# Cross-attention on one core: the first three steps, the normalisation and the last step rearranged

## What is computed

```python
h = (x - mean) * rsqrt(var + 1e-5) * gamma + beta      # x: 8 x 256 x 256
Q = (h @ Wq); K = (context @ Wk); V = (context @ Wv)   # context: 8 x 256 x 192, 16 heads of 64
attn = softmax(einsum('bihd,bjhd->bhij', Q, K), axis=-1) * 64 ** -0.5
out = einsum('bhij,bjhd->bihd', attn, V).reshape(8, 256, 1024) @ Wo + bo
return x + out
```

## Time and profile before

| | |
|---|---|
| runs | 374.82, 373.36, 373.44 us; median 373.44 |
| profiled execution | 374.68 us, of which the span of its records is 372.9 us |
| TensorE (PE) | busy 356.7 us, 96% of the span |
| VectorE (DVE) | busy 245.6 us, 66% |
| ScalarE (ACT) | busy 252.6 us, 68% |
| GpSimd (POOL) | busy 161.1 us, 43% |
| transfers | 10.39 MB, mean 28 GB/s |

### The profile page before, as it was taken

The page is one execution under the profiler, slowest core; times in us unless marked ns, Lnnn a source line. Parts: engine busy times, 40 slices in busy tenths (PEclk is TensorE's granted clock), DMA queues, the critical chain, the costliest instruction groups (busy, mean ns, idle before and its releaser), DMA issues.

```text
span 372.9 us, 8902 instructions
## 1 busy us (share of the span) xinstructions
PE 356.7 (96%) x3122; PEld 308.4 (83%) x3122; DVE 245.6 (66%) x534; ACT 252.6 (68%) x757; POOL 161.1 (43%) x314
## 2 busy tenths in 40 slices
PE   5896999999999999999999999999999999999984
PEld 4776888988888888888889888889888888988863
DVE  5877576675668656595656866676665956566552
ACT  5776866677766667776667777666776766677761
POOL 6437772445532373332624445324733335333330
PEclk9998999999999999999999999999999999999999
DMA  6940010020002000020000200010000000000000
GB/s 173 262 130 1 5 49 2 0 80 1 2 2 60 20 0 0 0 77 0 0 1 0 77 0 0 0 48 29 0 0 0 28 2 0 3 2 29 3 0 30
DMA packets 10135, 10.39 MB, mean 28 GB/s; under 512 B 864, under 2 KB 9056, under 8 KB 10112
## 3 DMA queue, kind: packets, MB, share of 16 engines
q1 hardware_dynamic: 9728, 9.77, 9.1%
q0 software_dynamic: 112, 0.13, 0.4%
q10 hardware_dynamic: 272, 0.20, 0.2%
HBM read 8.00 MB, written 2.10 MB: 27 GB/s over the span
## 4 chain that ended last, share of the span: by engine, by line
PE 91%; DVE 3%; ACT 3%; POOL 1%; issue 1%; POOLq 0%; DVEq 0%
PE st_ps L705 15%; PE mix_ps L642 15%; PE o_ps L693 13%; PE st_ps L623 13%; PE w_ps L672 12%; PE w_ps L661 11%; PE w_ps L724 10%; ACT prob L381 2%; PE w_ps L606 1%; PE w_ps L598 1%; DVE qk_lo L523 1%; DVE w_lo L442 1%; PE o_ps L593 1%; POOL w_lo L264 1%; DVE neg_max L510 1%
## 5 line engine op out<-in xcount | busy, mean ns | idle before, releaser
L292 POOL TENSOR_SCALAR prob<-prob,inv 128x256 f32<-128x256 f32 x256 | 121.6, 491 | 162.2 <-DVE inv L517 162.2
L381 ACT ACTIVATE prob<-st_ps,neg_max 128x256 f32<-128x256 f32 x256 | 118.6, 474 | 26.4 <-DVE neg_max L510 26.2
L510 DVE TENSOR_REDUCE neg_max<-st_ps 128x2 f32<-128x512 f32 x128 | 82.6, 684 | 35.4 <-PE st_ps L623 35.1
L425 ACT ACTIVATE prob_t<-st_ps 128x512 f32<-128x512 f32 x64 | 38.4, 599 | 49.7 <-PE st_ps L705 49.7
L575 DVE COPY prob_t<-st_ps 128x512 f32<-128x512 f32 x64 | 44.3, 692 | 37.0 <-PE st_ps L705 33.5
L642 PE MATMUL mix_ps<-prob_t,v_sb 128*64 128x256 f32 x512 | 62.3, 385 | 0.1
L705 PE MATMUL st_ps<-ident,prob 128*128 128x128 f32 x512 | 61.8, 274 | 0.0
L705 PEld LDWEIGHTS st_ps<-ident,prob 128*128 128x128 f32 x512 | 57.4, 142 | 0.1
L523 DVE TENSOR_TENSOR qk_lo<-w_ps,qk_hi 128x512 fp32r<-128x512 f32 x64 | 44.0, 688 | 17.6 <-ACT qk_hi L391 17.1
L381 ACT ACTIVATION_READ_ACCUMULATOR prob<-st_ps,neg_max 128x1 f32 x256 | 52.8, 206 | 0.0
L642 PEld LDWEIGHTS mix_ps<-prob_t,v_sb 128*64 128x64 f32 x512 | 34.0, 136 | 18.2 <-issue 0.3
(11 more groups left out here) (70 smaller groups left out, 579.5 us busy)
## 6 DMA issues: line engine op xcount, KB each, us to landing
x_in<-in_x_dram SPq DMA_DIRECT2D x8, 256.0 KB, 3.0
out_dram<-y_sb SPq DMA_DIRECT2D x8, 256.0 KB, 2.2
c_in<-in_ctx_dram SPq DMA_DIRECT2D x7, 192.0 KB, 2.9
w_raw<-in_L_xattn_Wo_dram SPq DMA_DIRECT2D x4, 256.0 KB, 7.6
w_raw<-in_L_xattn_Wk_dram SPq DMA_DIRECT2D x4, 128.0 KB, 4.8
w_raw<-in_L_xattn_Wq_dram SPq DMA_DIRECT2D x4, 128.0 KB, 3.3
w_raw<-in_L_xattn_Wv_dram SPq DMA_DIRECT2D x2, 256.0 KB, 7.0
w_raw<-in_L_xattn_Wv_dram SPq DMA_DIRECT2D x4, 128.0 KB, 6.6
```

The lines of the kernel that those rows point to most:

```text
L292: last = nc.gpsimd.tensor_scalar(prob[:, e, r, :], prob[:, e, r, :], inv[:, e, r:r + 1], SCALE, ALU.mult, ALU.mult)
L381: last = nc.scalar.activation(prob[:, e, r, :], st_ps[e][:, r * ROWS:(r + 1) * ROWS], ACT.Exp, bias=neg_max[:, e, r:r + 1], accum_out=sums ...
L510: nc.vector.tensor_reduce(neg_max[:, e, :], st_ps[e][:, :].rearrange("p (r j) -> p r j", r=RT), AX, ALU.max, negate=True).then_inc(max_rea ...
```

## The change

Six things are different.

- The quarters of K and Q: the second half of their columns comes as two quarters, 24 pieces of weights in place of 20. More of the low parts of late pieces are made by GpSimd (`LO_POOL`), and they stand at other places in the engines' orders.
- TensorE waits for the high parts ahead of the first pass of a projection, and for the low parts only ahead of the pass that reads them.
- In step 0 K and Q of step 1 are written to `mix_ps` and `o_ps` in place of `w0_ps` and `w1_ps` (`qk_banks`), and their first pass stands ahead of the scores of step 0. The second V goes to `w1_ps`, the second context to `o_ps`.
- Six of the eighteen transposes of the identity that open the kernel (`keep_warm`) are gone.
- The normalisation of the later sequences (`norm`) stands behind `keys_lo(1)` on VectorE and no longer ahead of `mix_lo`; the statistics of sequence 1 are taken in step 0 ahead of the copies of the probabilities.
- In the last step each pair has a bank of its own, its high and low parts are made apart, `o_ps` is added to `x_bias` early (`y_part`), and the two halves of the last result are added and stored apart, one from SyncE's queue and one from ScalarE's.

VectorE's, ScalarE's and SyncE's loops begin at step 3, TensorE's at step 2 as before. The diff, cut to its core:

```diff
-    LOOP_FROM, LOOP_STEPS, LOOPS = 2, 2 * PER_SEQ, 3
+    LOOP_STEPS, LOOPS = 2 * PER_SEQ, 3
...
-    PIECES = [(i, 0, QUART) for i in QK_TILES] + [(i, QUART, PIECE) for i in QK_TILES]
-    PIECES += [(i, 0, PIECE) for i in (V0, V0 + 1)]
-    PIECES += [(i, PIECE, INNER) for i in QK_TILES]
-    PIECES += [(O0, 0, PIECE)]
-    PIECES += [(i, PIECE, INNER) for i in (V0, V0 + 1)]
-    PIECES += [(O0, PIECE, INNER), (O0 + 1, 0, PIECE), (O0 + 1, PIECE, INNER)]
-    FOR_QK = {0: (2, 4), 2: (6, 8), 4: (12, 14)}
+    def quarter(n):
+        return [(i, n * QUART, (n + 1) * QUART) for i in QK_TILES]
+    PIECES = quarter(0) + quarter(1) + [(i, 0, PIECE) for i in (V0, V0 + 1)]
+    PIECES += quarter(2) + [(O0, 0, PIECE)] + [(i, PIECE, INNER) for i in (V0, V0 + 1)]
+    PIECES += quarter(3) + [(O0, PIECE, INNER), (O0 + 1, 0, PIECE), (O0 + 1, PIECE, INNER)]
+    FOR_K = {0: 2, 2: 6, 4: 12, 6: 19}
+    FOR_Q = {0: 4, 2: 8, 4: 14, 6: 21}
     FOR_V = {0: 10, 1: 17}
-    FOR_O = {0: 15, 1: 18, 2: 19, 3: 20}
-    LO_VECTOR = (0, 4, 5, 8, 9, 10, 11, 14, 15, 16)
-    LO_POOL = (1, 2, 3, 6, 7, 12, 13, 17, 18, 19)
-    HI_LATE = {0: (10, 11), 1: (14, 15, 16)}
-    LO_VECTOR_LATE = {0: (10, 11), 1: (14, 15, 16)}
-    LO_POOL_LATE = {0: (12, 13), 1: (17, 18, 19)}
+    FOR_O = {0: 15, 1: 22, 2: 23, 3: 24}
+    LO_VECTOR = (0, 4, 5, 8, 9, 13, 16)
+    LO_POOL = (1, 2, 3, 6, 7, 10, 11, 12, 14, 15, 17, 18, 19, 20, 21, 22, 23)
...
+        def qk_banks(u):
+            return (mix_ps, o_ps) if u == 0 else (w0_ps, w1_ps)
...
+        def high_ready(engine, n):
             engine.wait_ge(w_hi_ready, n)
...
+        def low_ready(engine, n):
+            engine.wait_ge(w_lo_ready, before(n, LO_VECTOR))
+            engine.wait_ge(w_lo_pool_ready, before(n, LO_POOL))
...
-                if b is not None:
+                if u == LAST - 1:
+                    sp.wait_ge(y_ready, SEQS)
+                    sp.dma_start(y_v[SEQS - 1, :, 0, :], y_sb[:, b % 2, 0, :])\
+                        .then_inc(y_free[b % 2], 16)
...
-            pool.dma_start(bo_b[:, :], b_o.partition_broadcast(P)).then_inc(bo_in, 16)
             for n in (1, 2, 3, 6, 7):
                 weight_lo(n)
+            pool.dma_start(bo_b[:, :], b_o.partition_broadcast(P)).then_inc(bo_in, 16)
...
+                if u == 1:
+                    weight_lo(14)
...
-                for n in LO_POOL_LATE.get(u, ()):
+                        if e == 1 and u in (1, 2):
+                            weight_lo({1: 15, 2: 21}[u])
+                for n in {0: (10, 11, 12), 1: (17, 18, 19, 20), 3: (23,)}.get(u, ()):
                     weight_lo(n)
-                if u == 1:
+                b = of_seq(u, SPLIT_H, 1)
+                if b is not None:
+                    hidden_lo(b)
+                if u == 2:
+                    weight_lo(22)
...
-                if 1 <= u < STEPS:
-                    values_out(u)
+                if 2 <= u < STEPS:
+                    values_out(u, w0_ps)
...
+                if u in (1, 2):
+                    weight_hi({1: 15, 2: 21}[u])
+                if u == STEPS:
+                    for a in range(BATCH):
+                        act.wait_ge(mixed, u + a)
+                        nc.scalar.activation(mix_hi[:, a, :], (mix_ps, w0_ps)[a][:, 0:ROWS],
+                                             ACT.Copy).then_inc(mix_hi_ready, 1)
+                elif 1 <= u < STEPS:
...
                 if u == 0:
-                    values_out(0)
-                for n in HI_LATE.get(u, ()):
-                    weight_hi(n)
+                    values_out(0, w0_ps)
+                    weight_hi(10)
+                    weight_hi(11)
+                    values_out(1, w1_ps)
+                if u == 1:
+                    weight_hi(16)
                 if 0 <= u < STEPS:
...
-                if u == 1:
-                    for n in (17, 18, 19):
-                        weight_hi(n)
-            walk(act, step)
+                        if u == 0 and e == 0:
+                            weight_hi(12)
+                            weight_hi(13)
+                for n in {1: (17, 18, 19, 20), 2: (22, 23)}.get(u, ()):
+                    weight_hi(n)
+            walk(act, step, 3)
+            act.wait_ge(y_ready, SEQS + 1)
+            act.dma_start(y_v[SEQS - 1, :, 1, :], y_sb[:, 1, 1, :]).then_inc(y_free[1], 16)
...
+                if u == STEPS:
...
+                    nc.vector.tensor_tensor(y_sb[:, 1, :, :].rearrange("p a b -> p (a b)"),
+                                            o_ps[:, :],
+                                            x_bias[:, 1, :, :].rearrange("p a b -> p (a b)"),
+                                            ALU.add).then_inc(y_part, 1)
+                if u == LAST - 1:
+                    dve.wait_ge(y_part, 1)
+                    for r in range(RT):
+                        dve.wait_ge(o_added, STEPS + r)
+                        nc.vector.tensor_tensor(y_sb[:, 1, r, :], (w1_ps, st_ps[0])[r][:, 0:D],
+                                                y_sb[:, 1, r, :], ALU.add).then_inc(y_ready, 1)
...
-                b = of_seq(u, NORM, 1)
-                if b is not None:
-                    dve.wait_ge(x_turned, b + turns(2))
-                    norm(b, turns)
-                if 1 <= u <= STEPS:
+                if u == STEPS:
+                    for a in range(BATCH):
+                        dve.wait_ge(mix_hi_ready, u + a)
+                        nc.vector.tensor_tensor(mix_lo[:, a, :], (mix_ps, w0_ps)[a][:, 0:ROWS],
+                                                mix_hi[:, a, :].bitcast(fp32), ALU.subtract)\
+                            .then_inc(mix_lo_ready, 1)
...
+                b = of_seq(u, NORM, 1)
+                if b == 1:
+                    norm(1, turns)
                 keys_lo(1)
-                for n in LO_VECTOR_LATE.get(u, ()):
-                    weight_lo(n)
+                if u == 0:
+                    statistics(1, turns)
+                if u == 1:
+                    weight_lo(16)
+                if b is not None and b >= 2:
+                    dve.wait_ge(x_turned, b + turns(2))
+                    norm(b, turns)
...
-                b = of_seq(u, STATS, 1)
+                        if u == 0 and e == 1:
+                            weight_lo(13)
...
+                    own_bank = w == STEPS - 1 and a == 1
+                    ps, first = (w0_ps, 0) if own_bank else (mix_ps, a * ROWS)
...
+                                ps[h * HALF:(h + 1) * HALF, first:first + ROWS],
                                 v_sb[:, w // RT % 2, j, p * P + h * HALF:p * P + (h + 1) * HALF],
...
+                for part in parts:
+                    if t in FOR_K:
+                        (high_ready, low_ready)[part](pe, FOR_K[t])
+                    for w, i, k in (passes[:CT], passes[CT:])[part]:
                         nc.tensor.matmul(ps[:, 0:ROWS], w[:, i, cols], c_t[:, b % 2, k, :],
...
+                if t in FOR_Q:
+                    high_ready(pe, FOR_Q[t])
+                if t == 0:
+                    pe.wait_ge(h_hi_first, 1)
+                    pe.wait_ge(h_second, 2)
+                elif p == 0:
+                    pe.wait_ge(h_lo_ready, DT * b + DT + turns(4))
+                for n, (w, h) in enumerate(((w_hi, h_hi), (w_lo, h_hi), (w_hi, h_lo))):
+                    if n == 1 and t in FOR_Q:
+                        low_ready(pe, FOR_Q[t])
+                    if n == 2 and t == 0:
+                        pe.wait_ge(h_lo_ready, DT)
...
+            def last_output():
+                for a in range(BATCH):
+                    pe.wait_ge(mix_lo_ready, STEPS + a)
+                    o, cols = divmod(PAIRS - BATCH + a, GROUP)
+                    cols = slice(cols * D, (cols + 1) * D)
+                    for r in range(RT):
+                        passes = ((mix_hi, w_hi), (mix_lo, w_hi), (mix_hi, w_lo))
+                        for n, (m, wt) in enumerate(passes):
+                            last = nc.tensor.matmul(
+                                (w1_ps, st_ps[0])[r][:, 0:D], m[:, a, r * P:(r + 1) * P],
+                                wt[:, O0 + o, cols], start=a == 0 and n == 0,
+                                stop=a == BATCH - 1 and n == 2, skip_group_check=True)
+                        if a == BATCH - 1:
+                            last.then_inc(o_added, 1)
             def turn(u, turns):
...
+                ps = w1_ps if n == 1 else w0_ps
...
-                if n == 1:
-                    pe.wait_ge(v_ready, 1)
-                else:
-                    pe.wait_ge(qk_lo_ready, BATCH * max(n, 1) + 1 + turns(16))
+                    high_ready(pe, FOR_V[g])
+                pe.wait_ge(qk_lo_ready, n + 1 if n < RT else BATCH * n + 1 + turns(16))
                 passes = context_products(V0)
                 for m, (w, i, k) in enumerate(passes):
-                    last = nc.tensor.matmul(w0_ps[:, :], c_t[:, b % 2, k, j * P:(j + 1) * P],
```

(22 more changed lines are left out.)

147 lines of the change are left out of this document (71 added, 76 removed).

## The result

The changed kernel takes **364.47 us** (median of 4 runs, 364.39 to 364.68), the one before 373.40 in the same comparison (373.36 to 374.82): a ratio of 0.9744, 95% interval 0.9722 to 0.9765. The profiled execution took 364.5 us with a span of 362.6; before, 374.68 and 372.9. The difference is 10.2 us where the sum had 7.9.

The account below looks back on a forecast made before the run. TensorE's own queue bounds the middle, so gains lie at start and end: 374.68 - 6.5 - 1.5 + 0.1 = 366.8 us profiled, 373.44 - 4.8 - 1.5 + 0.1 = 367.2 against the median; forecast 367.1, range 365.7 to 369.5.

Parts of the forecast that it names:

- Step D: The middle, from step 2: moved normalisation, loops and later transfers cost nothing; GpSimd's piece in step 2 costs 0.1 us.
- steps of unchanged length: A sign in the profile after that the prediction is right: the kernel's steps last as long as before.
- Step C: Step 1: waits of 1.02 and 2.17 us and 1.7 us of slow clock go, 0.2 returns; step 2 starts 6.5 earlier.
- Rival 1: In the opening the clock falls all the same, costing 1.7 us: 368.8 us, chance 0.12.
- Step A: Up to step 0's scores: they start at 12.15 us, 0.65 earlier; the removed transposes give no more than this.
- Step B: Step 0: the second half of step 1's scores starts near 23.15 us for 25.00, gain so far 1.8 us.
- Rival 2: Step 0 gains nothing, by late quarters or ScalarE's queue: 368.9 us, chance 0.13; with step 1's waits back, near 372, 0.05.
- `bo`'s later transfer: In the middle: it meets a buffer needed a full step later, so it costs nothing.
- the rule to coalesce: Loading K and Q: smaller pieces transfer slower, so the last quarters land up to 1.4 us later, 3.4 by the skill's page.
- rival 3: Middle: the moved normalisation delays `prob_t` six times; at 1.09 us each 373.6 us, slower above 1.4 each; chance 0.04.
- Step E: The end: halved copies, adds and stores issue the last store near 368.9 us for 370.30; gain taken as 1.5 us.
- The change of the loops: In the middle: loops that begin at another step meet buffers needed a full step later, so they cost nothing.

Follow-up runs that it names:

- e1: The changed kernel with the normalisation of sequences 2 to 7 back ahead of `mix_lo` on VectorE: 366.38 us, ratio 0.9788.
- e2: The kernel before with only the normalisation of sequences 2 to 7 moved behind `keys_lo(1)`: 372.99 us, ratio 0.9957.
- e8: The changed kernel with the low parts of pieces 14 and 15 made by VectorE at the end of step 1 again: 368.33 us, ratio 0.9841.
- e4: The changed kernel with the six transposes of the identity back between K and Q: 364.75 us, ratio 0.9743.
- e11: The changed kernel with piece 13's low part made by GpSimd and piece 21's two parts at the end of step 1: 363.84 us, ratio 0.9724.
- e3: The changed kernel with TensorE's loop begun at step 3, as the others', in place of step 2: 374.11 us, ratio 0.9989.

## Why the prediction was wrong

Its mechanisms held at the start and the end; one term put at nothing was not nothing, and the sum for the profiled execution was 2.3 us short.

- **Step D failed, where it says of the moved normalisation "nothing".** It gives 1.6 us (1.6 in the steps' lengths, 1.5 to 1.9 in e1, 1.3 to 1.6 in e2). The prediction looked only at what the normalisation would meet at its new place, and never at whom it held up at the old one: `mix_lo`, read by TensorE at once. The ground for not looking was the first sentence on the middle, "a queue of TensorE's own work". 149.96 busy of 150 us is no proof of that, since 0.16 us of each such wait lies under the modelled end of the product before it, and most of the rest is counted as work of the first product behind it. The sign "steps of unchanged length" failed with it.
- **Step C was 0.6 us short**, for the same reason in part. The bracketed waits of 1.02 and 2.17 us are each 0.16 longer when measured from start to start, and the first product behind the 1.02 also runs 0.07 longer: 0.4 us. The other 0.2 us are the wait for the last scaled head that I put in; it did not come, as heads 2 and 3 were scaled by 31.0.
- Step C's mechanism held: both waits went (e8 brings the longer one back; the one of 1.02 us has no experiment of its own), and with them the clock's fall, 1.7 us of the profiled execution (from the output of step 1 to the scores of step 2 it was 6.54 us and is 4.84). Rival 1 is out: all nine runs of the changed kernel have a mean clock of 0.999 or 1.0. Taking the median of before for executions without the fall was right as well: over 44 runs the two groups lie 1.3 us apart, and their clocks differ as well. The size was not: the sum took 1.7 us out for 1.3, so against the median (367.2 for 364.47) it is 2.7 us short and not 2.3. Why the groups are nearer than 1.7, no run shows.
- Step A came within 0.1 us, and the claim that the transposes give nothing on top was right to 0.3 us in the medians (e4).
- Step B was right at its end (23.18 for 23.2), in part by luck: two misses cancel. ScalarE was 0.5 us ahead of its chain (the high part of piece 13 ended at 21.52 for 22.0), and the low part behind it took about twice what was put. The same operation takes 0.41 us at 10.22, with GpSimd idle, and 0.76 and 0.88 at 12.12 and 21.55, while GpSimd makes low parts too. No run tests that as the cause. e11 shows that TensorE's wait at 23.18 hung on this piece. VectorE's timeline after:

```profile
21.55 0.88 DVE L480 TENSOR_TENSOR w_lo<-w_raw,w_hi 128x256 fp32r<-128x256 f32 x1 [0.17 <-ACT w_hi L350]
22.35 0.68 DVE L638 COPY prob_t<-st_ps 128x512 f32<-128x512 f32 x1
```

- Rival 2 is out. ScalarE's high parts of pieces 8 and 9 ran at 12.47 without waiting for their transfers, and the last piece of weights landed at 22.95 us, 0.8 earlier than before (23.77) and not up to 1.4 or 3.4 later. The lower speed in the earlier trace rows is not that of small pieces: up to 9.5 us both kernels issue the same transfers from SyncE at the same times, yet from 5 to 10 us they ran at 199 GB/s before and 243 after. What differs there is the transfer of `bo`, issued by GpSimd at 6.27 before and at 13.42 after; V's first piece, issued at 6.8, landed 6.2 us after its issue before and 3.3 after. So `bo`'s later transfer, put at nothing, may have helped the start; I made no run with it alone. From 15 to 20 us, where the pieces do differ, it is 250 GB/s for 285. On this the rule to coalesce (the Trainium skill, DMA: Bandwidth & Descriptors, Rules for kernel authors) predicted a loss; the rate here is lower, but nothing waited for it.
- Step D's piece in step 2 cost 0.29 us for 0.1, inside its bounds. The normalisation at its new place holds up nothing, so rival 3 is out.
- Step E gave 1.87 us for 1.5, with its chain as forecast. From the last `mix` on, the second pair's output starts 2.88 us later (2.86 forecast), TensorE's last product ends at 3.87 (3.86) and the last store is issued at 4.41 (4.51). That the first pair's output starts earlier still, at 2.02, gains nothing, since the second pair's low part ends last. The part mis-sized is what follows the issue of the last store: 2.23 us for the 2.6 that the sum kept as an upper bound.

Together: 0.6 + 1.4 (1.6 less 0.2 for step 2) + 0.4, less 0.1 that lies outside the span, is the 2.3 us missing. The range (365.7 at its low end) missed by 1.2 us, less than the normalisation's 1.6: its bounds for that term had a loss at one end and no gain at the other.

The change of the loops was put at nothing, and is so. But e3 shows that this rested on luck: with TensorE's loop moved along with the others' to step 3, the result would have been "no change", and neither the prediction nor its rivals had that case.

## What to carry to other kernels

Before you call a stretch bound by its busiest engine, list the lengths of steps that should be alike, and look at start-to-start distances where two engines hand over; a busy share of 100% hid 0.23 to 0.29 us in each of six steps here. When an instruction is moved, price both ends, what it meets at the new place and what it stood ahead of at the old. After any edit that moves a loop in an engine's program, compare the instruction queue's packets and the steps behind each backward turn with those of the version before. Instructions added to move code are not free: look for them in the trace.
